# A mixture-of-experts block on one core: statistics and centred rows one step further ahead, and one product moved from DVE to POOL

## The chip, the cores and the metric

The kernel runs on one core of a Trainium2 chip, as one launch. The metric is the time of that launch on the device in microseconds (us). Engines are called as in the profile: PE (matrix products and transposes), DVE (vector), ACT (scalar), POOL (GpSimd), SP (only issues transfers).

## The reference, cut to what matters

The input x is 16 blocks of 512 rows of 256 numbers, all fp32. Each block has its own modulation rows, six of 256 numbers, made from a condition row.

```
mod = silu(c) @ wmod                       # sa, ca, ga, sb, cb, gb; |ga|, |gb| at least 0.25
h   = layernorm(x) * (1 + ca) + sa
x   = x + ga * linear_attention(h)         # causal, q and k through elu + 1, heads of 64
h   = layernorm(x) * (1 + cb) + sb         # the second modulation
n   = layernorm(h, rn_g, rn_b)
top two of 8 experts from n @ router_w.T + router_b, softmax over the two
x   = x + gb * sum of the two experts' gelu networks (256 -> 1024 -> 256) on layernorm(h)
```

So each row passes three layer norms: of x, of x after the attention, and of h. Each needs a mean and an inverse root of the variance.

## The kernel before

The work has two stages. The **routing stage** makes attention, second modulation and router choice for the 16 blocks and scatters the normed rows into lists, one list for each expert. The **expert stage** runs through 71 tiles of up to 256 listed rows. The diff touches the setup and the routing stage.

Each engine has its own instruction stream in a fixed order that is written out by hand, and the streams meet only in semaphores. The routing stage is a software pipeline (`pipeline`, L273) of 21 steps. In step i the engines work on several blocks: block i is projected (`project`), block i-1 gets its attention (`attend`), block i-2 the statistics of its new rows (`settle`), block i-3 the second modulation (`norm`), block i-4 its router scores and choice (`route`), block i-5 its places in the lists and the scatter (`place`). A helper pipeline beside it splits the experts' weights into two bf16 parts; in odd steps DVE makes the rest of the first weights (L940), in even steps that of the second (L946).

**Statistics.** DVE makes them in three groups: group 0 for the raw rows of block i+1, group 1 for block i-2 after attention, group 2 for the modulated rows of block i-3. For each there is `bn_stats` (L771) and `bn_aggr` (L779); one instruction adds epsilon for all groups (`ve`, L786), POOL raises it to the power -0.5 (`rs`, L544), and DVE makes the negative mean times that (`nm`, L803). ACT then writes the centred and scaled rows (`normalise`, L628): `xc` of block i at the head of its step, `xn2` of block i-3 and the normed rows of block i-4. PE transposes `xc` (L1322), ACT modulates it while it copies it from PSUM (`hT`, L664), and PE projects it (L1355).

**Second modulation.** DVE multiplies `xn2` by a broadcast row (L901, 128 partitions x 1024 elements), then adds another row (L908) and makes the statistics of group 2.

**Choice and places.** DVE finds the two best scores, makes two masks from them (`oh`, L1006) and their sum (`ohs`, L1009). PE sums the masks to ranks (L1341 to L1345). DVE adds the base (`cnt`, L1046), multiplies by the masks (`pick`, L1052), sums (L1059) and casts to `slot` (L1064). POOL issues eight indirect transfers for each block (L551), four ahead of the inverse root and four behind it. At the head of its step POOL makes `wog`, the output weights times a modulation row (L559, 64 partitions x 256 elements).

**Order on DVE in a step.** Wait for `nm`; statistics of group 1; ranks, picks and slots; the diagonal masks of the attention strips (`diag`, L886); statistics of group 0; the modulation product and sum; statistics of group 2; `ve`; the feature map (`phi`, L926), the running sum (`scan`, L930) and a product (`qz`, L932); `nm`; the rests of the weights; the new rows `x2` (L968); the choice.

**Loads.** SP loads block i+2 of x in step i (`load_x`, L364), blocks 0 and 1 at the start. All blocks of x stay in SBUF through the routing stage.

Of the kernel before, what the change touches and what calls it, by code (L numbers as in the profile page):

```python
# [23 lines left out]
P = 128  # L24
# [28 lines left out]
def adaln_moe_kernel(nc, x_d, wq_d, wk_d, wv_d, wo_d, rng_d, rnb_d, rw_d, rb_d, lng_d, lnb_d,  # L53
# [6 lines left out]
    with ctx:  # L60
# [192 lines left out]
        def used(i):  # L253

            if not isinstance(i, int):
                return slice(0, 3)
            return slice(0 if i < NB else 1 if i - 3 < NB else 2, 1 if i < 3 else 2 if i < 4 else 3)
# [30 lines left out]
        def _(sp):  # L288
            sp.dma_start(cin[:, :], c_d).then_inc(got_c, 16)
# [14 lines left out]

            sp.wait_ge(mod_step, 8)
# [58 lines left out]
            def load_x(i, half, r):  # L364
                if isinstance(i, int):
                    if i + 2 < NB:
                        sp.wait_ge(got_x[r], 16 * (half + 1))
                        sp.dma_start(resid[:, (i + 2) * NC:(i + 3) * NC, :], x_v[i + 2]).then_inc(got_x[r], 16)
                else:
                    sp.wait_ge(got_x[r], 16 * half + 16)  # L370
                    sp.dma_start(resid[:, ds((i + 2) * NC, NC), :], x_v[ds(i + 2, 1)]).then_inc(got_x[r], 16)
# [120 lines left out]
        def _(pool):  # L492
# [42 lines left out]
            def inverse_root(i, r):  # L535

                pool.wait_ge(ve_s, i + 1)

                wait_past(pool, xc_s, upto(i - 1))
                wait_past(pool, xn2_s, upto(i - 4))  # L540
                wait_past(pool, nrm_s, upto(i - 5))
                wait_past(pool, nm_s, i - 1)
# [73 lines left out]
        def _(act):  # L616
# [13 lines left out]

            def step(i, half, r, project, attend, settle, norm, route, place):
                if project or norm or route:
                    act.wait_ge(nm_s, i + 1)
                if project:
                    act.wait_ge(got_x[r], 16 * half + 16)
                    wait_past(act, xT_s, i)
                    normalise(lambda c: xc[:, c, :], rows(i), r, 0, xc_s)
# [4 lines left out]
                if project and r == 1:  # L642
                    act.wait_ge(b1p_s, half + 1)
                    wait_past(act, b1_out, 32 * half)
                    hold(act, "act")
                    a.activation(b1rows, Q[0:H + 1, :], ACT.Copy).then_inc(b1r_s, 1)
                if norm:
# [9 lines left out]
                if project:  # L657

                    act.wait_ge(xT_s, i + 1)
                    act.wait_ge(modc_s, i + 1)  # L660
                    wait_past(act, proj_s, i)
                    hold(act, "act")
                    for k in range(NK):
                        last = a.activation(hT[:, k, :], TR[k][:, :], ACT.Identity,  # L664
                                            bias=modc[:, r, 2 + k:3 + k], scale=modc[:, r, k:k + 1])
                    last.then_inc(hT_s, 1)
# [88 lines left out]
        def _(dve):  # L755
# [32 lines left out]
            def stats_before(i):  # L788

                if not isinstance(i, int):  # L790
                    return 3 * i - 4
                return min(i + 1, NB) + min(max(i - 2, 0), NB) + min(max(i - 3, 0), NB)

            def neg_mean_rstd(i, r):

                dve.wait_ge(rs_s, i + 1)

                wait_past(dve, xc_s, upto(i - 1))
# [23 lines left out]
            var_eps(0, 1)  # L822
# [32 lines left out]
            dve.wait_ge(rb_ps, 1)  # L855
            dve.wait_ge(got_r, 32)
            dve.wait_ge(base_set, 1)
            v.tensor_tensor(rbias[:, :], rbias[:, :], S[1][:, 0:E], ALU.add).then_inc(setup_done, 1)
            dve.wait_ge(setup_done, 1)

            v.tensor_copy(lge[:, :], lngb[:, 0, :]).then_inc(lge_s, 1)

            def step(i, half, r, project, attend, settle, norm, route, place):
                taken = stats_before(i)
                dve.wait_ge(nm_s, i + 1 if not isinstance(i, int) else min(i + 1, NB + 4))
                if settle:
                    dve.wait_ge(x2_s, i - 1)
                    hold(dve, "dve")
                    stats(rows(i - 2), 1)
                if place:  # L870
# [16 lines left out]
                if project and not (isinstance(i, int) and i == NB - 1):  # L887
                    if r == 0:
                        dve.wait_ge(got_x[1], 16 * half + 16)
                    else:  # L890
                        dve.wait_ge(got_x[0], 16 * half + 32)
                    hold(dve, "dve")
                    stats(rows(i + 1), 0)
                if norm:

                    b, q = i - 3, 1 - r
                    dve.wait_ge(got_cs[q], 16 * (half if q == 0 else half - 1))
                    dve.wait_ge(xn2_s, b + 1)
                    wait_past(dve, nrm_s, b - 1)
                    hold(dve, "dve")  # L900
                    v.tensor_tensor(h2[q], xn2, csB[:, q, D:2 * D].unsqueeze(1).to_broadcast([P, NC, D]), ALU.mult).then_inc(h2m_s, 1)  # L901
                if project and not (isinstance(i, int) and i == NB - 1):
                    moments(0, taken)
                    taken = taken + 1
                if norm:
                    b, q = i - 3, 1 - r
# [26 lines left out]
                if project or attend or norm:  # L933
                    neg_mean_rstd(i + 1, 1 - r)
# [12 lines left out]

                if attend:
# [312 lines left out]
        def _(pe):  # L1261
# [27 lines left out]
            def router_bias():  # L1289
# [5 lines left out]
                pe.wait_ge(setup_done, 1)  # L1295
# [8 lines left out]
            def step(i, half, r, project, attend, settle, norm, route, place):  # L1304
# [214 lines left out]
```

## Time and profile before

| | us |
|---|---|
| three runs | 1122.92, 1125.62, 1125.95; median 1125.62 |
| the profiled execution | 1125.48 |
| its span | 1123.6 |

| engine | busy us | share of the span |
|---|---|---|
| PE | 988.9 | 88% |
| DVE | 889.1 | 79% |
| POOL | 573.6 | 51% |
| ACT | 542.9 | 48% |

The shares are means over two unlike stages. The routing stage takes the first third of the span and the expert stage, in which PE is nearly always busy, the rest. The granted clock of PE is a mean of 0.92 of full speed, with 0.8 to 0.9 in most slices of the routing stage. A row of a timeline has the start in us from the span's start, the duration in us, the engine, the line, the operation, what it writes and reads, and how many instructions are merged; brackets give the engine's idle time before it and what ended it.

### The profile page before, as it was taken

The numbers are of one execution on the slowest core, as the hardware profiler recorded it, in microseconds if no ns is written. First come the engines' busy times: TensorE is split into PE (matmuls) and PEld (weight loads), VectorE is DVE, ScalarE is ACT, GpSimd is POOL, SyncE is SP. The second block draws the span as 40 slices with busy tenths as digits, with TensorE's granted clock in tenths as the row PEclk, the third lists the DMA queues.
The fourth block names the chain that finished last, engine by engine and source line by source line (L and its number), as shares of the span: only waits on it lengthen the run. The fifth ranks groups of instructions, "written<-read, shape, count | busy, mean of one in ns | idle before, by whom it ended". The sixth has DMA issues, their size and how long they took to land.

```text
span 1123.6 us, 31567 instructions
## 1 busy us (share of the span) xinstructions
PE 988.9 (88%) x8116; PEld 806.3 (72%) x8117; DVE 889.1 (79%) x3010; ACT 542.9 (48%) x1123; POOL 573.6 (51%) x478
## 2 busy tenths in 40 slices
PE   5777879887945099999999999999999999999997
PEld 1334545554534088888888888888888888888875
DVE  5578999999985567777877877877877877877776
ACT  1668787878843134434444443444443443444443
POOL 2121666666667536655455445445445445545543
PEclk8798888888965599999999999999999999999999
DMA  4465777876869466665565555566555556566453
GB/s 134 133 227 194 237 230 260 291 271 212 315 233 401 122 185 132 137 123 92 96 118 98 106 112 104 98 109 99 94 108 103 90 108 108 87 120 122 88 100 49
DMA packets 162626, 169.80 MB, mean 151 GB/s; under 512 B 89340, under 2 KB 136968, under 8 KB 158472
## 3 DMA queue, kind: packets, MB, share of 16 engines
q1 hardware_dynamic: 129736, 114.24, 36.5%
q0 software_dynamic: 32832, 54.88, 25.3%
q8 instruction: 25, 0.41, 0.2%
q14 instruction: 33, 0.27, 0.1%
HBM read 94.67 MB, written 62.78 MB: 140 GB/s over the span
## 4 chain that ended last, share of the span: by engine, by line
PE 66%; issue 8%; DVE 8%; POOL 6%; ACT 2%; DMA 1%; POOLq 0%; DVEq 0%; SPq 0%; ACTq 0%
PE banks L1440 32%; PE banks L1452 31%; POOL lists L551 5%; PE banks L1334 2%; DVE st L771 2%; POOL rs L544 2%; DVE store L968 1%; PE banks L1322 1%; ACT rowbuf L628 1%; DVE mv L779 1%; ACT store L712 1%; DVE rowbuf L908 1%; DMA out<-rowbuf,ydst 0%; DVE store L926 0%; DVE ix L1001 0%
## 5 line engine op out<-in xcount | busy, mean ns | idle before, releaser
L1440 PE MATMUL banks<-nhl,store 128*128 128x256 bf16 (+1 forms) x3408 | 450.5, 268 | 28.0 <-DMA nhl<-xhl 24.8
L740 ACT ACTIVATE gf<-banks,b1t 128x256 f32<-128x256 f32 (+1 forms) x568 | 263.0, 463 | 429.1 <-PE banks L1440 411.7
L1452 PE MATMUL banks<-store 128*128 x3240 | 448.0, 273 | 0.5
L1440 PEld LDWEIGHTS banks<-nhl,store 128*128 x3408 | 324.1, 98 | 71.0 <-issue 30.1
L587 POOL DMA_INDIRECT out<-rowbuf,ydst x135 | 223.7, 1657 | 294.1 <-DVE rowbuf L1222 222.0
L1452 PEld LDWEIGHTS banks<-store 128*128 128x128 bf16 x3240 | 310.5, 98 | 41.9 <-issue 1.8
L1231 DVE CAST store<-gf 128x256 bf16<-128x256 f32 (+1 forms) x568 | 180.5, 318 | 130.7 <-ACT gf L740 99.3
L1233 DVE TENSOR_TENSOR store<-gf,store 128x256 bf16<-128x256 f32 (+1 forms) x568 | 234.7, 413 | 19.5
L551 POOL DMA_INDIRECT lists<-store,slot x128 | 141.0, 1102 | 96.3 <-issue 49.0
L578 POOL DMA_INDIRECT store<-y_rows,ygb x135 | 135.2, 1001 | 63.3 <-issue 51.8
L544 POOL TENSOR_TENSOR rs<-ve,mhalf 128x12 f32<-128x12 f32 (+2 forms) x20 | 39.0, 1950 | 84.6 <-DVE ve L786 84.5
L628 ACT ACTIVATE rowbuf<-store,nm,rs 128x256 f32<-128x256 f32 x128 | 66.1, 588 | 23.5 <-DVE nm L803 23.3
L1222 DVE SCALAR_TENSOR_TENSOR rowbuf<-rowbuf,yw,store 128x256 f32<-128x256 f32 x135 | 59.4, 479 | 0.2 <-DVE rowbuf L1212 0.2
L1322 PE MATMUL banks<-ident,rowbuf 128*128 128x128 f32 x128 | 25.1, 360 | 31.8 <-ACT rowbuf L628 31.8
L1334 PE MATMUL banks<-store,vT 64*128 64x512 f32 (+3 forms) x128 | 38.4, 662 | 16.5 <-DVE store L968 8.5
L1183 DVE TENSOR_TENSOR xhl<-rowbuf,xhl 128x512 bf16<-128x512 f32 (+1 forms) x71 | 46.6, 658 | 7.7 <-ACT xhl L731 7.7
L731 ACT ACTIVATE xhl<-rowbuf 128x512 bf16<-128x512 f32 (+1 forms) x71 | 42.6, 600 | 18.4 <-DMA rowbuf<-lists 18.4
L1212 DVE TENSOR_TENSOR rowbuf<-banks,b2t 128x256 f32<-128x256 f32 x135 | 50.8, 416 | 0.7 <-PE banks L1452 0.7
L1322 PEld LDWEIGHTS banks<-ident,rowbuf 128*128 128x128 f32 x128 | 19.7, 183 | 41.1 <-ACT rowbuf L628 39.5
L771 DVE BATCH_NORM_STATS2 st<-store 128x6 f32<-128x256 f32 x128 | 44.8, 412 | 2.3 <-DMA store<-in_L_attn_x 2.0
L1355 PE MATMUL banks<-store,wqk 128*128 128x512 f32 x64 | 42.0, 790 | 3.0 <-ACT store L664 3.0
L1334 PEld LDWEIGHTS banks<-store,vT 64*128 64x128 f32 x128 | 23.2, 276 | 27.6 <-issue 24.5
(225 smaller groups left out, 970.0 us busy)
## 6 DMA issues: line engine op xcount, KB each, us to landing
rowbuf<-lists SPq DMA_DIRECT2D x64, 264.0 KB
store<-in_L_ffn_w SPq DMA_DIRECT2D x16, 1024.0 KB, 6.0
wsplit<-store SPq DMA_DIRECT2D x16, 1024.0 KB, 5.7
store<-wsplit SPq DMA_DIRECT2D x16, 1024.0 KB, 11.1
b2t<-in_L_ffn_b SPq DMA_DIRECT2D x71, 128.0 KB
store<-in_L_attn_x SPq DMA_DIRECT2D x16, 512.0 KB, 9.6
out<-store SPq DMA_DIRECT2D x16, 512.0 KB, 9.9
csB<-mod_rows SPq DMA_DIRECT2D x16, 256.0 KB, 4.0
```

The source lines that it names most:

```text
L544: g.tensor_tensor(rs[:, r, n, :], ve[:, n, :], mhalf[:, n, :], ALU.pow).then_inc(rs_s, 1)
L551: g.indirect_dma_start(list_d, bass.IndirectOffsetOnAxis(ap=slot[:, b % NR, t, c:c + 1], axis=0), nrm[:, b % NR, c, :], None).then_inc(sca ...
L578: g.indirect_dma_start(gbr[:, r, h, :], None, y_d[GBROW:GBROW + NB, :], bass.IndirectOffsetOnAxis(ap=ygb[:, r, h:h + 1], axis=0)).then_inc ...
L587: g.indirect_dma_start(out_rows, bass.IndirectOffsetOnAxis(ap=ydst[:, r, h:h + 1], axis=0), yt[:, r, h, :], None, compute_op=ALU.add).then ...
L628: last = a.activation(out(c), src(c), ACT.Identity, bias=nm[:, r, n, c:c + 1], scale=rs[:, r, n, c:c + 1])
L740: a.activation(gf[:, c % 2, 0:halves(j) * P], MM[c % 2][:, 0:halves(j) * P], ACT.Gelu, bias=b1t[:, r, c:c + 1]).then_inc(gf_s, 1)
L771: last = v.bn_stats(st[:, n, c, :], src(c))
L1231: v.tensor_copy(gh[:, c, cols], gf[:, c % 2, cols]).then_inc(gh_s, 1)
L1233: v.tensor_tensor(gl[:, c, cols], gf[:, c % 2, cols], gh[:, c, cols], ALU.subtract).then_inc(gl_s, 1)
L1334: last = t.matmul(SC[s], vT[at, q, s // 2 * P:(s // 2 + 1) * P], q_of[at, q, s * P:T], start=True, stop=True)
L1440: last = t.matmul(MM[c % 2][:, 0:halves(j) * P], w, nhl[:, r, m, 0:halves(j) * P], start=n == 0, stop=n == 5)
L1452: last = t.matmul(ACC[r][h][:, 0:D], g[:, c, h * P:(h + 1) * P], w, start=c == 0 and n == 0, stop=c == NI - 1 and n == 2)
```

## The change

Five things are edited.

1. In step i DVE makes the group 0 statistics of block i+2 (before: i+1), and it does so right behind those of group 1, ahead of ranks and slots. Setup makes two sets, for blocks 0 and 1. The counts in the waits go up by one.
2. ACT writes `xc` of block i+1 in step i, behind the attention output. It modulates and copies `hT` ahead of the wait for `nm`, and writes `xn2` behind it. Setup writes `xc` of block 0, and step 0 that of block 1.
3. POOL makes the modulation product, between `wog` and the first four scatters. It waits for `xn2` and for `ohs` of DVE's previous step. DVE keeps the sum (L908).
4. DVE makes `nm` behind the rests of the weights instead of ahead of them.
5. SP loads blocks 2 and 3 in setup and block i+3 in step i. The sum of the router's bias leaves the setup and is made in step 0; PE waits for it in step 1.

```diff
@@ sync
+            for b in range(2, 4):
+                load_block(b)
             sp.wait_ge(mod_step, 8)
...
             def load_x(i, half, r):
+                if 0 < i < NB - 3:
+                    load_block(i + 3)
@@ gpsimd
             def inverse_root(i, r):
-                pool.wait_ge(ve_s, i + 1)
+                pool.wait_ge(ve_s, i + 2)
...
+            inverse_root(-1, 1)
             inverse_root(0, 0)
...
+                if norm:
+                    b, q = i - 3, 1 - r
+                    pool.wait_ge(got_cs[q], 16 * (half if q == 0 else half - 1))
+                    pool.wait_ge(xn2_s, b + 1)
+                    wait_past(pool, nrm_s, b - 1)
+                    wait_past(pool, ohs_s, i - 4)
+                    hold(pool, "pool")
+                    g.tensor_tensor(h2[q], xn2, csB[:, q, D:2 * D].unsqueeze(1).to_broadcast([P, NC, D]), ALU.mult).then_inc(h2m_s, 1)
                 if place:
@@ scalar
+            def centred(b, r):
+                act.wait_ge(got_x[b % 2], 16 * (b // 2) + 16)
+                wait_past(act, xT_s, b)
+                normalise(lambda c: xc[:, c, :], rows(b), r, 0, xc_s)
+            act.wait_ge(nm_s, 1)
+            centred(0, 1)
...
+                if project:
+                    act.wait_ge(xT_s, i + 1)
...
+                    last.then_inc(hT_s, 1)
+                if i + 1 < NB or norm or route:
+                    act.wait_ge(nm_s, i + 2)
                 if norm:
...
+                if i == 0:
+                    centred(1, 0)
...
+                if 0 < i < NB - 1:
+                    centred(i + 1, r)
@@ vector
-            var_eps(0, 1)
+            var_eps(-1, 1)
+            dve.wait_ge(got_x[1], 16)
+            dve.wait_ge(mv_s, 1)
+            hold(dve, "dve")
+            stats(rows(1), 0)
+            neg_mean_rstd(-1, 1)
+            dve.wait_ge(nm_s, 1)
+            dve.wait_ge(ve_s, 1)
+            moments(0, 1)
+            var_eps(0, 2)
             dve.wait_ge(mod_ps, 1)
...
                     stats(rows(i - 2), 1)
+                if i + 2 < NB:
+                    dve.wait_ge(got_x[r], 16 * half + 32)
+                    hold(dve, "dve")
+                    stats(rows(i + 2), 0)
                 if place:
...
-                    stats(rows(i + 1), 0)
                 if norm:
                     b, q = i - 3, 1 - r
                     dve.wait_ge(got_cs[q], 16 * (half if q == 0 else half - 1))
-                    dve.wait_ge(xn2_s, b + 1)
-                    wait_past(dve, nrm_s, b - 1)
-                    hold(dve, "dve")
-                    v.tensor_tensor(h2[q], xn2, csB[:, q, D:2 * D].unsqueeze(1).to_broadcast([P, NC, D]), ALU.mult).then_inc(h2m_s, 1)
...
-                if project or attend or norm:
-                    neg_mean_rstd(i + 1, 1 - r)
+                if i == 0:
+                    router_bias()
                 if project and r == 1:
...
                     v.tensor_tensor(wbuf[:, 0, 6144:8192], w2f, wbuf[:, 0, 4096:6144], ALU.subtract).then_inc(rest2_s, 1)
 
+                if project or attend or norm:
+                    neg_mean_rstd(i + 1, 1 - r)
@@ tensor
-                pe.wait_ge(setup_done, 1)
...
+                    if b == 0:
+                        pe.wait_ge(setup_done, 1)
```

## Rows read from the trace of the kernel before

**Rows 1.** The table by stretches of time: length, each engine's busy us, PE clock.
```profile
112.00:302.00 190.00, 157.81 (x908) 100.41 (x908) 179.37 (x674) 151.22 (x304) 122.35 (x100) 0.85 0.77 259
...
383.00:1123.60 740.60, 718.81 (x6648) 634.33 (x6648) 575.52 (x1832) 298.53 (x639) 375.44 (x286) 0.99 0.58 107
```

**Rows 2.** The timeline of POOL: start us, us, what, idle time before.
```profile
1.96 0.16 POOL L500 IOTA experts<- 128x8 f32 x1
...
113.32 1.20 POOL L551 DMA_INDIRECT lists<-store,slot  x1 [10.25 <-issue]
...
208.15 1.00 POOL L551 DMA_INDIRECT lists<-store,slot  x1 [4.92 <-DVE slot L1064]
209.46 1.72 POOL L551 DMA_INDIRECT lists<-store,slot  x1 [0.30 <-issue]
...
214.22 2.30 POOL L544 TENSOR_TENSOR rs<-ve,mhalf 128x12 f32<-128x12 f32 x1 [0.39 <-DVE ve L786]
...
222.57 0.73 POOL L559 TENSOR_TENSOR wog<-wo,gaB 64x256 f32<-64x256 f32 x1
226.75 1.00 POOL L551 DMA_INDIRECT lists<-store,slot  x1 [3.45 <-DVE slot L1064]
...
240.17 0.74 POOL L559 TENSOR_TENSOR wog<-wo,gaB 64x256 f32<-64x256 f32 x1
...
302.96 1.44 POOL L551 DMA_INDIRECT lists<-store,slot  x1 [4.01 <-issue]
...
321.24 1.76 POOL L551 DMA_INDIRECT lists<-store,slot  x1 [4.87 <-DVE slot L1064]
...
338.07 1.27 POOL L551 DMA_INDIRECT lists<-store,slot  x1 [3.59 <-DVE slot L1064]
...
350.15 1.11 POOL L551 DMA_INDIRECT lists<-store,slot  x1 [0.30 <-issue]
```

**Rows 3.** The timeline of DVE in a full even step.
```profile
206.12 0.19 DVE L1046 TENSOR_TENSOR cnt<-banks,base 128x32 f32<-128x32 f32 x1 [0.62 <-PE banks L1345]
...
206.35 0.22 DVE L1052 TENSOR_TENSOR pick<-oh,cnt 128x64 f32<-128x64 f32 x1
...
207.82 1.40 DVE L771 BATCH_NORM_STATS2 st<-store 128x6 f32<-128x256 f32 x4
209.13 1.21 DVE L901 TENSOR_TENSOR rowbuf<-rowbuf,csB 128x1024 f32<-128x1024 f32 x1
210.26 0.37 DVE L779 BATCH_NORM_AGGREGATE mv<-st 128x2 f32<-128x6 f32 x4
```

**Rows 4.** All instructions of line 559: shortest, median, longest in ns.
```profile
L559 POOL TENSOR_TENSOR wog<-wo,gaB x16: 723/742/1385, 35.4 to 315.6; 64x256 f32<-64x256 f32 x16
```

**Rows 5.** The timeline of DVE: two mask sums and one scan.
```profile
203.59 0.19 DVE L1009 TENSOR_TENSOR ohs<-oh 128x32 bf16<-128x32 f32 x1
...
214.84 1.22 DVE L930 TENSOR_TENSOR_SCAN zT<-onesf,store 64x512 f32<-64x512 f32 x1
...
222.72 0.64 DVE L1009 TENSOR_TENSOR ohs<-oh 128x32 bf16<-128x32 f32 x1
```

**Rows 6.** The timelines of ACT, PE and DVE in the first steps.
```profile
17.93 2.08 ACT L628 ACTIVATE rowbuf<-store,nm,rs 128x256 f32<-128x256 f32 x4 [14.97 <-DVE nm L803]
...
30.16 0.63 ACT L688 ACTIVATE ex<-ex 128x512 f32<-128x512 f32 x1
...
20.16 1.94 PE L1322 MATMUL banks<-ident,rowbuf 128*128 128x128 f32 x8 [1.51 <-ACT rowbuf L628]
...
38.00 1.97 PE L1322 MATMUL banks<-ident,rowbuf 128*128 128x128 f32 x8 [0.60 <-ACT rowbuf L628]
...
32.44 0.68 DVE L926 SCALAR_TENSOR_TENSOR store<-banks,ex 128x512 f32<-128x512 f32 x1
...
74.35 0.69 DVE L886 TENSOR_TENSOR store<-store,causal 128x512 f32<-128x512 f32 x1 [1.56 <-ACT store L672]
...
92.91 0.69 DVE L886 TENSOR_TENSOR store<-store,causal 128x512 f32<-128x512 f32 x1 [1.93 <-ACT store L672]
```

More of the change, by code:

```diff
@@ L256, in used @@
                 return slice(0, 3)
-            return slice(0 if i < NB else 1 if i - 3 < NB else 2, 1 if i < 3 else 2 if i < 4 else 3)
+            return slice(0 if i + 1 < NB else 1 if i - 3 < NB else 2, 1 if i < 3 else 2 if i < 4 else 3)
         def halves(j):
@@ L288, in _, with load_block @@
         def _(sp):
+            def load_block(b):
+                sp.wait_ge(got_x[b % 2], 16 * (b // 2))
+                sp.dma_start(resid[:, b * NC:(b + 1) * NC, :], x_v[b]).then_inc(got_x[b % 2], 16)
             sp.dma_start(cin[:, :], c_d).then_inc(got_c, 16)
@@ L364, in load_x @@
             def load_x(i, half, r):
[L365 to L371, printed above, removed]
+                if 0 < i < NB - 3:
+                    load_block(i + 3)
             def load_w1(e):
@@ L629, in normalise @@
                 last.then_inc(done, 1)
-            def step(i, half, r, project, attend, settle, norm, route, place):
[L632 to L637, printed above, removed]
+            def centred(b, r):
[4 more added lines that the diff above has]
+            centred(0, 1)
+            def step(i, half, r, project, attend, settle, norm, route, place):
                 if attend:
@@ L646, in step @@
                     a.activation(b1rows, Q[0:H + 1, :], ACT.Copy).then_inc(b1r_s, 1)
+                if project:
+                    act.wait_ge(xT_s, i + 1)
+                    act.wait_ge(modc_s, i + 1)
+                    wait_past(act, proj_s, i)
+                    hold(act, "act")
+                    for k in range(NK):
+                        last = a.activation(hT[:, k, :], TR[k][:, :], ACT.Identity,
+                                            bias=modc[:, r, 2 + k:3 + k], scale=modc[:, r, k:k + 1])
+                    last.then_inc(hT_s, 1)
+                if i + 1 < NB or norm or route:
+                    act.wait_ge(nm_s, i + 2)
                 if norm:
@@ L656, in step @@
                     a.activation(dex[:, :], dl[:, :], ACT.Exp).then_inc(dex_s, 1)
[L657 to L666, printed above, removed]
+                if i == 0:
+                    centred(1, 0)
                 if attend:
@@ L788, in stats_before @@
             def stats_before(i):
-                if not isinstance(i, int):
-                    return 3 * i - 4
-                return min(i + 1, NB) + min(max(i - 2, 0), NB) + min(max(i - 3, 0), NB)
+                return min(i + 2, NB) + min(max(i - 2, 0), NB) + min(max(i - 3, 0), NB)
             def neg_mean_rstd(i, r):
-                dve.wait_ge(rs_s, i + 1)
-                wait_past(dve, xc_s, upto(i - 1))
+                dve.wait_ge(rs_s, i + 2)
+                wait_past(dve, xc_s, upto(i))
                 wait_past(dve, xn2_s, upto(i - 4))
@@ L854, in _, with router_bias @@
             v.tensor_copy(ef[:, 0, 0:1], base[:, 0:1]).then_inc(base_set, 1)
-            dve.wait_ge(rb_ps, 1)
-            dve.wait_ge(got_r, 32)
             dve.wait_ge(base_set, 1)
-            v.tensor_tensor(rbias[:, :], rbias[:, :], S[1][:, 0:E], ALU.add).then_inc(setup_done, 1)
-            dve.wait_ge(setup_done, 1)
+            hold(dve, "dve")
             v.tensor_copy(lge[:, :], lngb[:, 0, :]).then_inc(lge_s, 1)
+            def router_bias():
+                dve.wait_ge(rb_ps, 1)
+                dve.wait_ge(got_r, 32)
+                v.tensor_tensor(rbias[:, :], rbias[:, :], S[1][:, 0:E], ALU.add).then_inc(setup_done, 1)
+                dve.wait_ge(setup_done, 1)
             def step(i, half, r, project, attend, settle, norm, route, place):
                 taken = stats_before(i)
-                dve.wait_ge(nm_s, i + 1 if not isinstance(i, int) else min(i + 1, NB + 4))
+                dve.wait_ge(nm_s, min(i + 2, NB + 5))
                 if settle:
@@ L869, in step @@
                     stats(rows(i - 2), 1)
+                if i + 2 < NB:
+                    dve.wait_ge(got_x[r], 16 * half + 32)
+                    hold(dve, "dve")
+                    stats(rows(i + 2), 0)
                 if place:
@@ L886, in step @@
                     v.tensor_tensor(diag, diag, causal[:, :].unsqueeze(1).to_broadcast([P, NC, P]), ALU.mult).then_inc(diag_s, 1)
[L887 to L891, printed above, removed]
-                    hold(dve, "dve")
-                    stats(rows(i + 1), 0)
                 if norm:
@@ L897, in step @@
                     dve.wait_ge(got_cs[q], 16 * (half if q == 0 else half - 1))
-                    dve.wait_ge(xn2_s, b + 1)
-                    wait_past(dve, nrm_s, b - 1)
-                    hold(dve, "dve")
-                    v.tensor_tensor(h2[q], xn2, csB[:, q, D:2 * D].unsqueeze(1).to_broadcast([P, NC, D]), ALU.mult).then_inc(h2m_s, 1)
-                if project and not (isinstance(i, int) and i == NB - 1):
+                if i + 2 < NB:
                     moments(0, taken)
@@ L905, in step @@
                 if norm:
-                    b, q = i - 3, 1 - r
                     dve.wait_ge(h2m_s, b + 1)
```

4 lines of the change are left out of this document (2 added, 2 removed).

## The prediction

> **What bounds the kernel now.** I read the table by stretches first. The last 740 us are the expert stage, where PE is busy 97% of the time at the full clock; nothing of the change lies in it [rows 1]. The change can only move its start, so I look for the time of the last scatter. In the stretch of the full batch steps, 112 to 302 us, DVE is busy 179 of 190 us, PE 158, ACT 151 and POOL 122 [rows 1]. DVE is thus the engine that sets the pace, and the reader is to see in the timelines where the others wait for it. POOL starts a step's scatters at 113.32 in the first step that has any and at 302.96 ten steps later, so 18.96 us a step [rows 2]. Between them it waits 4.92 and 3.45 us for DVE's slots, in an even and an odd step [rows 2]. From one wait to the end of the next wog product POOL needs 15.15 us in the even step (208.15 to 223.30) and 14.16 us in the odd one (226.75 to 240.91), 14.66 in the mean [rows 2]. So POOL has 4.2 us a step to spare, and that is the whole room for a new POOL product.
>
> **Taking the product from DVE.** L901 starts at 209.13 and the next DVE instruction 1.13 us later: 1.13 us less DVE work in 16 steps [rows 3]. DVE also waits 0.62 us for PE's ranks in even steps [rows 3]; with the statistics of the block after next put ahead of the ranks (1.31 us from start to start [rows 3]) that wait is filled, some 0.3 us a step. DVE alone could then do a step in 18.96 - 1.13 - 0.31 = 17.5 us, and in 17.2 when the wog product no longer falls on its mask sums (next paragraph).
>
> **What POOL pays.** wog is 64x256 and takes 0.723 us at least, 0.742 in the median and 1.385 at most over 16 [rows 4]. The new product has 1024 elements in each partition, four times as many. If all of 0.742 goes by element it takes 2.97 us. An IOTA of 8 elements takes 0.16 us [rows 2], which is about what an instruction costs in itself: (0.742 - 0.16) x 4 + 0.16 = 2.5 us, my value. The lower end is the DVE's own 1.21 us [rows 3], the upper four times the longest wog, 5.5 us. *GPSIMD Engine Reference* in the Trainium skill, section 3.1, gives 4497 ns for a two-input product of 2048 elements, about 2.3 us for half of it; no run here shows that size yet, and by it the sum below would fall by 0.2 us a step.
>
> **The wait that comes with it.** With room 4.2 and price 2.5 the product seems free, but the two engines hold each other up. ohs, a sum of two SBUF inputs, takes 0.19 us at 203.59 with POOL idle and 0.64 us at 222.72, and then it ends at 223.36, 0.06 after the wog product (222.57 to 223.30) [rows 2, 5]. So DVE's two-input operation waits until POOL's product is over. The other way round, POOL's second scatter takes 1.72 us instead of about 0.96, and it starts in the middle of L901 [rows 2, 3]. The new product is released by ohs. Behind it on DVE come two small copies and both sets of statistics, which have one input each, and then pick, which has two. From ohs to pick that is 2.76 us in the step shown (203.59 to 206.35 [rows 3, 5]), less 0.62 of waiting, plus 1.31: about 3.4, or 3.2 from the end of ohs. A product that starts at once ends at 2.6 and disturbs nobody. A late one holds pick. From the start of pick to the first scatter it is 1.80 us (206.35 to 208.15) [rows 2, 3]. POOL's circle is then: 0.1 to start, 2.5 for the product, 1.8 for pick, slots and the way to POOL, and POOL's own work. That work is 14.66 less the 0.39 us in which the power waited for ve [rows 2] (in the new order ve is ready first), less about 0.35 because L946 stands elsewhere (its hold on the scatters falls in even steps only), plus 0.2 because L908 now falls on the first scatter from its beginning: 14.1, bounds 13.9 and 14.7. The circle is 18.5 us, longer than DVE's 17.2. If the product started at once, POOL would be done at 3.2 + 1.8 + 14.1 = 19.1 us after ohs, 1.9 us too late for a step of 17.2; so from the second such step on it does come late, pick is held by about 1.3 us a step, and POOL's circle sets the pace. Ten steps of 18.96 become ten of 18.5: 4.6 us gained, instead of the 17 that DVE's busy time promises. The other cuts on DVE disappear in the hold.
>
> *SBUF — State Buffer* in the Trainium skill, section Who interferes with whom, says of this that a DVE operation with two SBUF inputs and a POOL operation that reads SBUF exclude each other for the whole instruction. The ohs row agrees. The scan at 214.84 does not: it has two SBUF inputs, lies inside the power of 2.30 us at 214.22 and takes 1.22 us all the same [rows 2, 5]. The measurement decides, so the hold is certain for a product with many elements only as far as wog shows it.
>
> **The early steps.** Here DVE is not full and a chain is cut. ACT centres block 0 only when DVE has gone through the modulation rows, and PE stands until 20.16 for it; ACT has then waited 14.97 us for nm [rows 6]. With the centring released before those rows, PE starts behind its own transposes, 1.5 us earlier (PE's wait ahead of 20.16 is 1.51). ex is ready at 30.16 + 0.63 = 30.8, but DVE takes it at 32.44 because it is making statistics [rows 6]; these move into DVE's idle time before, another 1.6. PE's wait of 0.60 for xc at 38.00 goes [rows 6]. In the steps at 53 and 63 us the chain runs through x2 and the scores and I count nothing. In the two steps with the product but without scatters (diag at 74.35 and 92.91) DVE waits 1.56 and 1.93 us for the strips [rows 6]; the 1.31 us of statistics fit there, and 1.13 go to POOL, which is idle: 2.44 twice, 4.9. Sum 1.5 + 1.6 + 0.6 + 4.9 = 8.6. At the first scatter step the statistics stand ahead of the slots and cost 1.31 - 0.62 = 0.7. First scatter 7.9 us earlier; ends: 5 if ACT or PE is late next in the two middle steps, 10 if wog's holds on DVE go there as well. Blocks 2 and 3 are loaded some 15 us earlier, into a stretch where the queue waits for the modulation rows; I give that nothing. The router bias sum moves behind step 0's work and PE waits for it only in step 1, nothing either.
>
> **The end.** The last scatters are POOL's chain: starts at 302.96, 321.24, 338.07, 350.15 [rows 2]. The product falls in the first two waits: the first interval is 18.28 with a wait of 4.87, so POOL works 13.4; plus 0.1 + 2.5 + 1.8 is 17.8, so -0.5. The second is 16.83 with a wait of 3.59, 13.2 of work, 17.6 with the product, +0.8. Ahead of 350.15 POOL has only the 0.30 us that lie ahead of every scatter, so the third costs its whole 2.5. Sum +2.8. Moving nm behind the weight remainders frees DVE while POOL raises the power, but POOL's queue sets the end, so nothing.
>
> **The sum.** -7.9 - 4.6 + 2.8 = -9.7, and with the holds of wog in the early steps (up to 2, I take 1) -10.7. The profiled execution takes 1125.48 for a span of 1123.6, and the median of the runs is 1125.62, the same within 0.2. Forecast 1115.
>
> **Rivals.** *DVE sets the pace.* The product doesn't hold pick, or only in part, as the power doesn't hold the scan. Then a step is 17.2, POOL needs 0.1 + 2.5 + 14.1 = 16.7 and fits: -7.9 - 17.6 + 2.5 = -23, 1103. For it speaks DVE's 179 of 190 us, against it the 0.64 us of ohs. *Nothing moves.* The product takes 2.97 and both old delays of the scatters stay: 0.1 + 2.97 + 1.8 + 14.66 = 19.5, +5.7 in ten steps, +4.3 at the end, -7.9: +2, 1127 at worst and 1123 if only one of them holds. *Slower: a slow POOL product.* Place: between ohs and pick, in every step from the second scatter step on. Each us over 2.5 costs ten steps and three at the end, 13 us in all, so it decides from 2.5 + 10/13 = 3.3 us on. At 4.0 us it gives 1115 + 19 = 1134, at 5.5, four times the longest wog, 1154. For it: wog's 1.385 when DVE holds it up; against it: its median lies at its minimum, and the stretch after ohs has no two-input operation. *The early gain is not there*: the steps with centring ahead have another late input; then -2, 1123.
>
> **Chances.** Forecast (1108 to 1121) 0.55, DVE sets the pace 0.17, nothing moves or no early gain 0.16, slower by the slow product 0.12. The range 1100 to 1127 leaves out the slow product and the best of the DVE case. A change of 0.3% (3.4 us) is about what a measurement here can tell: faster 0.75, the same 0.12, slower 0.13.
>
> **What would show it.** Right: POOL's new product near 2.5 us; its start later than ohs by 1 us or more in the full steps; pick drawn out to about a us or more and ending just after the product; scatter starts 18.5 us apart; first scatter near 105.5; PE without a wait for xc. Wrong: scatter starts 17.2 apart with pick at 0.2 us (first rival), or a product over 3.3 us (the slower one). DVE's busy time falls by about 16 x 1.13 = 18 us less the holds in every case and proves nothing.

## The result: slower by 0.6%, and the profile after

The kernel after takes 1131.88 us (median of 4 runs, 1127.96 to 1133.22), the kernel before 1124.41 us (4 runs, 1122.92 to 1125.95): ratio 1.0061, 95% interval 1.0044 to 1.0077. I had forecast 1115, so the sign was wrong, and the time lies outside the range. The profiled execution of after is its fastest one, 1127.96 us with a span of 1126.2; the rows below explain +2.6 us of span, and the end of this section says what the slower runs have in addition.

The table by stretches (length, busy us of PE, PEld, DVE, ACT and POOL with their instructions, PE clock, busy share of the DMA engines, GB/s):
```profile
112.00:302.00 190.00, 154.99 (x865) 96.14 (x865) 170.01 (x632) 146.71 (x293) 152.84 (x108) 0.82 0.73 251
...
383.00:1126.20 743.20, 718.65 (x6648) 634.22 (x6648) 575.91 (x1835) 298.49 (x639) 377.30 (x288) 0.99 0.59 107
```
Beside [rows 1], DVE has 9 us less and POOL 30 us more, of which ten products explain 24: POOL's other instructions have grown too. The expert stage is as long as before. The first scatter stands at 106.63 instead of 113.32 (-6.7), from it to the first scatter ten steps later it is 194.52 us instead of 189.64 (+4.9), and from there to the first expert matmul 95.87 instead of 91.36 (+4.5). Together +2.7. The rows are of after, and the last one is of before:
```profile
106.63 2.04 POOL L554 DMA_INDIRECT lists<-store,slot  x1 [2.22 <-issue]
...
301.15 1.75 POOL L554 DMA_INDIRECT lists<-store,slot  x1 [1.67 <-DVE slot L1087]
...
397.02 4.39 PE L1464 MATMUL banks<-nhl,store 128*128 128x256 bf16 x24 [24.56 <-DMA nhl<-xhl]
```
```profile
394.32 4.47 PE L1440 MATMUL banks<-nhl,store 128*128 128x256 bf16 x24 [24.82 <-DMA nhl<-xhl]
```

Where the ten steps lose, the timeline of POOL shows (start us, us, instruction, idle time before); it answers to [rows 2]:
```profile
184.29 2.01 POOL L554 DMA_INDIRECT lists<-store,slot  x1 [1.74 <-DVE slot L1087]
...
190.56 2.30 POOL L546 TENSOR_TENSOR rs<-ve,mhalf 128x12 f32<-128x12 f32 x1
...
198.59 2.36 POOL L570 TENSOR_TENSOR rowbuf<-rowbuf,csB 128x1024 f32<-128x1024 f32 x1
202.69 2.01 POOL L554 DMA_INDIRECT lists<-store,slot  x1 [1.74 <-DVE slot L1087]
...
208.95 4.41 POOL L546 TENSOR_TENSOR rs<-ve,mhalf 128x12 f32<-128x12 f32 x1
...
219.09 2.36 POOL L570 TENSOR_TENSOR rowbuf<-rowbuf,csB 128x1024 f32<-128x1024 f32 x1
223.19 2.01 POOL L554 DMA_INDIRECT lists<-store,slot  x1 [1.74 <-DVE slot L1087]
...
229.46 3.40 POOL L546 TENSOR_TENSOR rs<-ve,mhalf 128x12 f32<-128x12 f32 x1
```
The circle is there: product 2.36, then 1.74 until DVE's slots let the next scatter start, then POOL's own work until the next product. From 184.29 to 202.69 it is 18.40 us, my 18.5. From 202.69 to 223.19 it is 20.50, and nearly all of the difference is one instruction: the power of 12 elements takes 4.41 us instead of 2.30. Four of the ten intervals are 20.5 with a power of 4.41; four are 18.2 to 18.4; one odd step has a power of 3.40 and 19.51; and in the last interval, 19.55, the power is one of 8 elements and takes 3.78 where the unheld ones take 1.67. Ten times 18.4 would be 184.

The timeline of DVE at the same time, which answers to [rows 3, 5]:
```profile
190.51 2.55 DVE L961 SCALAR_TENSOR_TENSOR store<-store,lge 128x1024 bf16<-128x1024 f32 x2
...
196.56 0.19 DVE L1032 TENSOR_TENSOR ohs<-oh 128x32 bf16<-128x32 f32 x1
...
197.07 2.71 DVE L791 BATCH_NORM_STATS2 st<-store 128x6 f32<-128x256 f32 x8
199.70 0.17 DVE L1069 TENSOR_TENSOR cnt<-banks,base 128x32 f32<-128x32 f32 x1
199.79 1.20 DVE L1051 TENSOR_SCALAR d<-dex 128x4 f32<-128x4 f32 x1
200.90 0.21 DVE L1075 TENSOR_TENSOR pick<-oh,cnt 128x64 f32<-128x64 f32 x1
...
202.65 1.19 DVE L929 TENSOR_TENSOR rowbuf<-rowbuf,csB 128x1024 f32<-128x1024 f32 x1
...
208.19 0.69 DVE L953 TENSOR_TENSOR store<-store,zT 64x512 f32<-64x512 f32 x1
208.91 2.29 DVE L967 TENSOR_TENSOR store<-store 128x2048 bf16<-128x2048 f32 x1
...
229.41 2.48 DVE L961 SCALAR_TENSOR_TENSOR store<-store,lge 128x1024 bf16<-128x1024 f32 x2
```
L967, the rest of the second weights (the remainder of the even steps; L961 is that of the odd ones), starts at 208.91, the power at 208.95. The power ends at 213.36, 2.16 us after the remainder, so nearly all of its 2.3 us of work came after the remainder was over. In the odd step L961 starts at 190.51 and the power at 190.56, and here the power is at its 2.30 and L961 the one that is drawn out a little: its two pieces take 2.55 us, and 2.48 at 229.41, where the power is the one of 3.40. That power was held by the first piece (1.1 us) and not by the second. L929 starts at 202.65 and stretches the scatter of 202.69 to 2.01 us. The two engines meet in this way in every step, since L953 holds the fourth scatter (207.56, 1.37 us for 0.96) until DVE is through with it, and the power and the remainder then start in the same moment.

The end, POOL again:
```profile
322.49 3.07 POOL L554 DMA_INDIRECT lists<-store,slot  x1 [0.30 <-issue]
...
349.65 2.37 POOL L570 TENSOR_TENSOR rowbuf<-rowbuf,csB 128x1024 f32<-128x1024 f32 x1
352.18 2.04 POOL L554 DMA_INDIRECT lists<-store,slot  x1 [0.17 <-issue]
```
The product at 349.65 costs its whole length, as foreseen (the interval before 352.18 is 14.50 for 12.08). Not foreseen: a scatter of 3.07 us, which falls on L967 of the last step that has it (322.42 to 324.71), and one of 2.04, which falls on L929 (it starts at 352.12). An undisturbed scatter takes 0.96.

The start of the first steps, PE and DVE, answering to [rows 6]:
```profile
18.03 1.97 PE L1344 MATMUL banks<-ident,rowbuf 128*128 128x128 f32 x8
...
27.69 0.69 DVE L947 SCALAR_TENSOR_TENSOR store<-banks,ex 128x512 f32<-128x512 f32 x1 [0.62 <-ACT ex L706]
```
PE starts 2.1 us earlier and DVE takes ex 4.75 us earlier.

The other executions take up to 1133. Part of that is more long powers in odd steps: the profile of a repeat (after_again, span 1128.9, +2.7) has two of 3.4 us instead of one. Its ten intervals take 1.2 us more, the way from there to the first expert matmul 0.5, the expert stage 0.8, and its first scatter is at 106.78. The 4 us between the profiled execution and the median are thus explained in part only.

In the four traces with this order on DVE (after, its two repeats and rest2_stt below) the remainder starts 0.03 to 0.06 us ahead of the power at every meeting. The even one (L967) holds the power in 20 of 20, the odd one (L961) in 8 of 24. rest2_stt, in which both have the same form, has the same split, so it isn't the form; why they differ stays open.

### The profile page after: what moved, and what is told of

Its sections match the earlier page's. It is cut to its first block, busy times and chain, and to the rows that moved or that the text cites. A ratio compares the mean times of both kernels' runs of the same rounds, so it can differ in the third digit from the quotient of the medians.

```text
span 1126.2 us, 31567 instructions
## 1 busy us (share of the span) xinstructions
PE 987.9 (88%) x8116; PEld 803.7 (71%) x8117; DVE 885.4 (79%) x2996; ACT 544.5 (48%) x1123; POOL 624.5 (55%) x495
## 4 chain that ended last, share of the span: by engine, by line
PE 64%; DVE 12%; POOL 8%; issue 6%; DMA 1%; ACT 1%; POOLq 0%; DVEq 0%; SPq 0%; ACTq 0%
PE banks L1464 31%; PE banks L1476 31%; POOL lists L554 5%; POOL rs L546 3%; DVE st L791 3%; DVE store L991 2%; DVE d L1051 1%; DVE store L961 1%; PE banks L1358 1%; DVE zT L951 1%; DVE ix L1024 1%; DVE rowbuf L929 0%; DVE mv L799 0%; DVE mx L1014 0%; DMA out<-rowbuf,ydst 0%
## 5 line engine op out<-in xcount | busy, mean ns | idle before, releaser
L554 POOL DMA_INDIRECT lists<-store,slot x128 | 144.5, 1129 | 57.6 <-issue 32.5
L546 POOL TENSOR_TENSOR rs<-ve,mhalf 128x12 f32<-128x12 f32 (+2 forms) x21 | 50.3, 2396 | 49.3 <-DVE ve L806 48.9
L570 POOL TENSOR_TENSOR rowbuf<-rowbuf,csB 128x1024 f32<-128x1024 f32 x16 | 37.8, 2361 | 20.9 <-ACT rowbuf L639 12.2
L1379 PE MATMUL banks<-store,wqk 128*128 128x512 f32 x64 | 45.8, 856 | 1.8 <-ACT store L668 1.8
L1431 PE MATMUL banks<-wog,store 128*128 128x257 f32 x128 | 38.9, 458 | 3.6 <-ACT store L719 3.6
```

Source lines behind the costliest of these rows:

```text
L554: g.indirect_dma_start(list_d, bass.IndirectOffsetOnAxis(ap=slot[:, b % NR, t, c:c + 1], axis=0), nrm[:, b % NR, c, :], None).then_inc(sca ...
```

## Experiments

The theory from this profile, H: a two-input operation of DVE and a POOL instruction that reads SBUF exclude each other; whoever is first makes the other wait. The product on POOL isn't slow, but it leaves POOL so little room that the power always meets the remainder. Rivals: the order of remainder and nm does it (O), the form of the remainder's instruction (F), something that only accompanies the long power, as PE's clock or transfers (C).

**The same kernel again, twice.**

> The changed kernel once more, to see what differs between its executions. Theory H (held operations): in even steps POOL's power waits behind the rest of the second weights (2.29 us, both inputs in SBUF), so it takes 4.41 us instead of 2.30; in odd steps power and the first piece of the rest of the first weights start within 50 ns of each other, and either may win, which is 1.1 us a step. So the scatter intervals alternate near 18.4 and 20.5 us, and more of the odd ones are 19.5 in a slower execution: 1128 to 1134 us, about 1131.5. Rival C (clock and transfers: PE's granted clock is 0.82 in the full steps instead of 0.85, and the loads come earlier): a slower execution has a lower clock and longer PE stretches, with the same intervals of the power.

> The kernel after, unchanged, so that the two runs behind it have it on their own chip. 1.004 to 1.008 of the kernel before; power 4.4 us in even steps; intervals 20.5 (even) and 18.4 or 19.5 (odd).

1130.46 us, ratio 1.0054 (1.0042 to 1.0066), and 1131.46, 1.0065 (1.0046 to 1.0084). The even intervals are 20.5 and the even powers 4.41 in both; in the second the first scatter is later too (108.21).

**nm ahead of the remainders again.**
```diff
+ if project or attend or norm: neg_mean_rstd(i + 1, 1 - r)   # ahead of the remainders, as in before
- if project or attend or norm: neg_mean_rstd(i + 1, 1 - r)   # behind them
```

> The changed kernel with nm ahead of the weight rests again (edit 4 undone). Theory H: the power is no longer held (2.30 us in all steps), but DVE now waits for it before the rests, so the rests fall behind it, hold one of the last four scatters by up to 1 us in even steps, and delay x2 and the mask sums by 2.3 us in odd steps. The product then waits for the mask sums; interval 19.4 in the mean as now, 1131 us (1127 to 1136). Rival O (edit 4 alone is what costs): the power at 2.30 us gives 2.1 us back in each even step, 10 to 12 us in all, 1120 us.

1133.94 us, 1.0090 (1.0075 to 1.0105): slower still, O falls. POOL and DVE:
```profile
212.59 2.30 POOL L546 TENSOR_TENSOR rs<-ve,mhalf 128x12 f32<-128x12 f32 x1
...
216.43 1.91 POOL L554 DMA_INDIRECT lists<-store,slot  x1 [0.30 <-issue]
```
```profile
215.07 0.22 DVE L821 SCALAR_TENSOR_TENSOR nm<-mv,rs 128x12 f32<-128x12 f32 x1 [2.55 <-POOL rs L546]
215.22 2.29 DVE L969 TENSOR_TENSOR store<-store 128x2048 bf16<-128x2048 f32 x1
```
All full powers are 2.30 now, but DVE stands still for 2.55 us for each, and the remainder falls on a scatter instead. Intervals are 19.2 to 20.7.

**The product back on DVE, all else as after.**
```diff
- g.tensor_tensor(h2[q], xn2, csB[...], ALU.mult).then_inc(h2m_s, 1)   # POOL, behind ohs
+ v.tensor_tensor(h2[q], xn2, csB[...], ALU.mult).then_inc(h2m_s, 1)   # DVE, where before has it
```

> The changed kernel with the modulation product back on DVE in its old place; all else of the change stays. Theory H: POOL has room again, the power starts when ve is ready and is over before the weight rests, so 2.30 us; d is not drawn out. DVE sets the pace at about 18.96 less 0.3 for the filled rank wait, 18.6; first scatter at 106.6 + 2.3 = 109; the end as before. -4.4 - 3.5 = -8: 1117 us, faster than before. Rival C: the product's place has nothing to do with it, the loss stays: 1126 to 1132 us.

1119.61 us, 0.9951 (0.9939 to 0.9964): faster than before. The other edits are good for 5 us, and the product's move takes away 11. POOL:
```profile
181.48 1.76 POOL L554 DMA_INDIRECT lists<-store,slot  x1 [2.86 <-DVE slot L1083]
...
187.16 3.02 POOL L546 TENSOR_TENSOR rs<-ve,mhalf 128x12 f32<-128x12 f32 x1
```
and DVE:
```profile
186.86 1.22 DVE L947 TENSOR_TENSOR_SCAN zT<-onesf,store 64x512 f32<-64x512 f32 x1
```
POOL waits again, 2.86 us here, and so starts its power at another point of DVE's step: it is held 0.7 us, by the scan, and not 2.1 (I had expected no hold at all). Seven of the ten intervals are 17.8 to 18.4. In the longest one, 20.57, DVE waits 1.53 us for PE, whose granted clock is 0.75 there; that step is long through PE and not through POOL.

**The remainder in another form.**
```diff
- v.tensor_tensor(rest2, w2f, rounded, ALU.subtract)
+ v.scalar_tensor_tensor(rest2, w2f, 1.0, rounded, ALU.mult, ALU.subtract)
```

> The changed kernel with the rest of the second weights as one scalar_tensor_tensor (w2 times 1.0, minus the head) instead of a tensor_tensor; same two inputs in SBUF, same size. Theory H: any operation with two SBUF inputs holds the power, the form doesn't matter and only who is first: power 4.4 us as now in even steps, 1131 us. Theory F (the form matters: the rest of the first weights is a scalar_tensor_tensor and left the power at 2.30 in three of four odd steps): power 2.30 in even steps, 5 x 2.1 us less in ten steps and 1 to 2 at the end, 1119 us. Rival C: 1131 us.

1129.64 us, 1.0044 (1.0028 to 1.0060), the even power 4.42 us, interval 20.5. F falls.

**The product alone, in the kernel before**, on two chips.
```diff
- v.tensor_tensor(h2[q], xn2, csB[...], ALU.mult).then_inc(h2m_s, 1)
+ g.tensor_tensor(h2[q], xn2, csB[...], ALU.mult).then_inc(h2m_s, 1)   # on POOL, behind wog and ohs
```

> The kernel before, with nothing but the modulation product moved to POOL behind ohs. The power begins ahead of the scan and 2.7 us ahead of the remainder in the kernel before, so theory H expects no long hold there unless the engines shift against each other by those 2.7 us: POOL's circle is 0.1 + 2.4 + 1.8 + 14.1 to 14.7 = 18.4 to 19.0 us, the end costs 2.8 to 4.5, the first scatter is 1 to 2 us earlier: 1123 to 1130, between no change and slower. If the product's move alone is what makes the power fall together with the remainder (a phase that the circle forces on the two engines, whatever the order of the statistics), the power takes 4.4 us in some steps here too, and it is 1130 or more.

> The same kernel as product_alone, where the expert stage has its usual length. From its trace: last scatter at 388.1, 6.5 us behind that of the kernel before, nearly all of it in the last six steps (85.9 instead of 78.6 us), so 1.004 to 1.006 of the kernel before. A theory in which only the order of the statistics does the harm: 1.000 or less.

On the first of these chips the expert stage is longer (the kernel before takes 1154.15 us there), and I use only the traces up to the first expert matmul from it. There: 1154.65 us, 0.9993 (0.9977 to 1.0010). On the second: 1127.63 us, 1.0026 (1.0017 to 1.0035), less than the 1.004 expected. The full powers are 2.30 but for one of 3.03, and the ten steps take 187.68 us, 2.0 less than before: without the new order of the statistics the power starts ahead of the remainder and isn't held. The loss is at the end: from the first scatter ten steps on to the last scatter of all it is 85.6 us instead of 78.6 (that one is at 385.12 instead of 381.59). So the product alone costs 0.3% (nothing on the first chip), the rest alone gains 0.5%, and both together lose 0.5 to 0.7%: the sum of the two would be a gain of 0.2%, and some 0.8% comes from their meeting. The three ratios are from different chips, so the 0.8 is rough.

**The remainders in pieces of 512 elements**, on the same two chips (after ran on the second only).
```diff
- v.tensor_tensor(rest2[0:2048], ...)
+ for n in range(4): v.tensor_tensor(rest2[n * 512:(n + 1) * 512], ...)   # L961's two likewise in halves
```

> The kernel after, with the weight remainders cut: the two scalar_tensor_tensor of 1024 elements into four of 512, the tensor_tensor of 2048 into four of 512; same work, same order. Theory H (POOL's power and DVE's remainder, which start in the same moment, exclude each other; whoever is first makes the other wait to its end): the power then waits for one piece of some 0.55 us and no longer for 2.1, so it takes at most 2.9 us in even and odd steps, the scatter starts of the full steps are 18.4 to 19.0 us apart in both parities, and the time is 8 to 10 us under the kernel after, 1120 to 1123. Rival K (DVE keeps its place over instructions that follow each other without a gap): the power still takes 4.4 us in even steps and 1131 stays. Rival C (the even steps are long for another reason, PE's clock or a transfer, and the long power is a symptom): the power gets short and the even intervals stay near 20.5.

> The same kernel as rests_in_pieces (weight remainders in pieces of 512 elements), on a chip on which the expert stage has its usual length. Theory H: full steps of 18.4 to 19.0 us instead of 20.5 and 18.4 to 19.5 by turns, so 7 to 10 us under the kernel after, 0.997 to 1.000 of the kernel before. Theory C (the length of a step is set elsewhere): within 2 us of the kernel after.

1150.40 us, 0.9964 (0.9947 to 0.9981), and 1127.50, 1.0028 (1.0014 to 1.0041). Beside after on the second chip (1131.46) that is 4 us, not 7 to 10. POOL and then DVE of the second:
```profile
162.00 2.37 POOL L570 TENSOR_TENSOR rowbuf<-rowbuf,csB 128x1024 f32<-128x1024 f32 x1
168.95 2.01 POOL L554 DMA_INDIRECT lists<-store,slot  x1 [4.58 <-DVE slot L1093]
...
184.96 2.35 POOL L570 TENSOR_TENSOR rowbuf<-rowbuf,csB 128x1024 f32<-128x1024 f32 x1 [1.14 <-issue]
...
213.78 2.82 POOL L546 TENSOR_TENSOR rs<-ve,mhalf 128x12 f32<-128x12 f32 x1
```
```profile
160.66 3.76 DVE L1012 COPY lge<-lngb 128x4 f32<-128x4 f32 x1
...
185.00 2.40 DVE L1081 TENSOR_TENSOR pick<-oh,cnt 128x64 f32<-128x64 f32 x1
...
213.75 2.51 DVE L971 TENSOR_TENSOR store<-store 128x512 bf16<-128x512 f32 x4
```
The power at 213.78 waits for one piece, 0.5 us, and gets its turn between two: H, not the rival by which DVE keeps its place. From 188.97 on the steps are 18.56 and 18.94 by turns, with the power at 2.30 and 2.82, which is the forecast's circle; the interval follows the power, and C falls. The gain is lost ahead of that, in steps of 21.38 and 20.02: a COPY of 4 elements takes 3.76 us in the first of them, through the last scatter, wog and the product, and everything behind it is late. In the second the product starts late itself (1.14 us of idle time before it) and holds pick for 2.40 us.

**Half of the product on each engine, remainders in pieces.**
```diff
- g.tensor_tensor(h2[q], xn2, ...)
+ g.tensor_tensor(h2[q][:, 0:2, :], xn2[:, 0:2, :], ...)   # POOL
+ v.tensor_tensor(h2[q][:, 2:4, :], xn2[:, 2:4, :], ...)   # DVE
```

> As the run before, and of the modulation product only the first half (512 of 1024 elements) is made on POOL, the second on DVE behind ohs. Theory H: POOL's circle loses half of 2.36 us, about 1.2, DVE gains 0.6; a step then has some 17.4 us of POOL and 17.8 of DVE: intervals 17.8 to 18.2, the end cheaper by 3 times 1.2, in all 1114 to 1118, under the kernel before. A theory in which the product's length matters little because DVE or PE sets the pace anyway: the same as rests_in_pieces within 2 us.

A miss: 1154.32 us, 0.9998 (0.9981 to 1.0015), 4 us above the run with the whole product on POOL. POOL has time (it waits 4.59 us for the slots at 265.33), but DVE is held before it reaches them:
```profile
279.63 1.28 POOL L570 TENSOR_TENSOR rowbuf<-rowbuf,csB 128x512 f32<-128x512 f32 x1
```
```profile
278.39 2.56 DVE L1048 CAST store<-ix 128x4 f32<-128x4 uint32 x1
```
This cast ends at 280.95 and the half product at 280.91; between the cast's start and there POOL has wog (278.95, 0.74 us) and the half product, and the cast is held through both. In seven of the ten steps a cast or copy behind ohs takes 2.0 to 2.6 us; with the whole product (rests_in_pieces) that happens in one. The powers of the full steps are held too, at 2.9 to 3.0. That POOL meets the casts because the shorter product brings it to wog earlier is only argued.

**The remainders behind x2.**

```diff
- remainders, nm; den, lg, max, x2
+ den, lg, max, x2; remainders, nm      # the order on DVE
```

> The kernel after, with the weight remainders and nm moved behind the residual sum x2, so that DVE makes x2 while POOL raises the power. Theory H: the power is held by nothing or by the two pieces of x2 only, 2.30 to 3.0 us in every step; but the remainders come later and can hold a scatter (2.0 us more once in a step where one falls on it) and x2 comes 2.3 us earlier to PE. Intervals 18.4 to 19.5, time 1119 to 1127. Rival C: even intervals stay at 20.5 whatever the power takes.

1157.87 us, 1.0039 (1.0017 to 1.0060), no gain. The profiled execution is its fastest, 1151.39, so the rows show where a step's time goes but not what the median has in addition. POOL and DVE:
```profile
207.03 2.30 POOL L546 TENSOR_TENSOR rs<-ve,mhalf 128x12 f32<-128x12 f32 x1
209.52 2.91 POOL L554 DMA_INDIRECT lists<-store,slot  x1 [0.20 <-issue]
```
```profile
209.22 2.28 DVE L990 TENSOR_TENSOR store<-store 128x2048 bf16<-128x2048 f32 x1
```
The power is 2.30 in all full steps, and the interval here is still 20.28. That is C's number, but POOL's own instructions account for it: 2.11 less on the power, 1.95 more on the scatter on which the remainder now falls. POOL is busy throughout, and so the hold found a victim in each of the three places that the remainder has had.

**The product on POOL only while POOL is idle.**
```diff
- if norm:                  # POOL: product
+ if norm and i < 5:        # POOL: product; DVE makes it for i >= 5
```

> The kernel after with the product on POOL in the two steps that have no scatters (i < 5), and on DVE in the 14 others. Theory H: the product costs nothing where POOL is idle and a hold on its circle where it is not. First scatter as in the kernel after (106 to 107, 1.5 us before that of product_on_dve), intervals of 18.0 and 18.0 to 19.2 as in product_on_dve, the time 1 to 2 us under product_on_dve, 0.993 to 0.996 of the kernel before. If the early gain is lost again because DVE sets the pace of the first scatter steps: as product_on_dve, 0.995.

1113.88 us, 0.9909 (0.9889 to 0.9929): the best version, 11 us under before and 18 under after. First scatter at 105.37, eight of the ten intervals 17.8 to 18.4 and the others 18.6 and 20.9, and no product behind the last power. In the one of 20.9 DVE waits 1.69 us for PE at a granted clock of 0.76. POOL waits for DVE again:
```profile
216.94 1.76 POOL L554 DMA_INDIRECT lists<-store,slot  x1 [2.88 <-DVE slot L1092]
```
It is more than the 1 to 2 us over product_on_dve that I expected (another chip, ratios 0.9951 and 0.9909). 2.8 us of it are the first scatter (108.14 there), but 1.6 of these are there already when DVE takes ex of the third step (57.92 instead of 59.51), ahead of the first product, where the two kernels are the same; the product can account for the other 1.2. In the last intervals product_on_dve has 19.79 and 19.49 where this one has 17.79 and 16.71. The table by stretches for these two intervals, first of product_on_dve and then of this kernel:
```profile
293.39:313.18 19.79, 14.24 (x66) 10.82 (x66) 16.57 (x60) 11.69 (x25) 10.81 (x11) 0.57 0.63 225
313.18:332.67 19.49, 13.82 (x64) 11.29 (x64) 13.30 (x54) 7.26 (x16) 12.32 (x10) 0.50 0.67 225
```
```profile
289.69:307.48 17.79, 11.26 (x66) 8.55 (x66) 16.72 (x59) 11.66 (x25) 11.91 (x10) 0.72 0.62 211
307.48:324.19 16.71, 9.77 (x64) 8.01 (x64) 13.23 (x54) 7.26 (x16) 12.31 (x10) 0.70 0.83 304
```
The same PE work takes 14.24 us at a granted clock of 0.57 and 11.26 at 0.72; 0.50 is the lower of the two levels, 1.2 GHz. Why the one run got less clock there stays open. So of the 0.4% between the two versions only 1.2 us, 0.1%, has its cause shown; the gain over after (0.9909 and 1.0065 on the same chip) stands apart from that.

## Why the prediction was wrong

- *What bounds the kernel.* DVE, with room of 4.2 us on POOL: right, and it was the room that mattered. After, POOL sets the pace.
- *The product costs 2.5 us.* 2.36, at 16 of 16 places within 0.03. The figure of 4497 ns in *GPSIMD Engine Reference* in the Trainium skill, section 3.1, which the prediction names, is for an add; half of it, 2.25 us, is an estimate as near to the 2.36 as mine, on the other side. The slow product, my rival on the slower side, is not what happened.
- *The circle.* Right in form: product, slots, POOL's own work. It says 18.5, the odd steps have 18.4. The instruction that is held is `d`, which has one input, and not pick, but for one step (297.12, 2.46 us): the ten `d` have a median of 1206 ns, and 158 with the product on DVE. The sum is the same.
- *POOL's own work is 14.1, bounds 13.9 and 14.7.* **This step failed.** It is 14.30 in the odd steps (184.29 to 198.59) and 16.40 in the even ones (202.69 to 219.09). I had let it shrink by 0.35 us, since L946 "stands elsewhere"; instead the remainder, now L967, moved onto the power and holds it 2.1 us. Five such holds (four of 2.11, and 3.78 for 1.67) make 10.5 and the odd one 1.1, together 11.6. Without them the ten intervals would sum to 182.9, 2.1 under my 185.0: -4.6 + 11.6 - 2.1 = +4.9. That is 9.5 us over the forecast. The early steps are 2.2 over (-8.9 counted, with the 1 us for wog's holds, and -6.7 measured) and the end 1.7, together the way from -10.7 to the +2.7 of the profiled execution.
- *Why I let it pass.* I took the scan of [rows 5], which lies inside the power and isn't drawn out, as a case against the hold. But the power had begun first (214.22, the scan 214.84), and in the new order DVE is first. product_on_dve shows the difference with the same pair: scan at 186.86, power at 187.16, and the power takes 3.02. *SBUF — State Buffer* in the Trainium skill, section Who interferes with whom, which the prediction names, also says that issue order decides who blocks. The trace agrees where DVE is clearly first; with starts 0.03 to 0.06 us apart both outcomes occur.
- *The early steps, -7.9.* -6.7: near, but partly by luck. DVE takes ex 4.75 us earlier in step 0 and 5.2 earlier in the third step (forecast 3.1 and 3.7); the two steps with the product and no scatters then gain 3.2, not 4.9; and the first scatter step loses 1.8, not 0.7, since `d` is held there too (1.23 us at 103.22; in product_early_on_pool, without a product there, it takes 0.16 and the first scatter is 1.3 us earlier).
- *The end, +2.8.* +4.5. The third product is as priced (+2.4); the scatters of 3.07 and 2.04 us are holds that I hadn't counted (2.1 and 1.1). "POOL's queue sets the end, so nothing" was wrong for the order of remainder and nm, since the remainder now meets a scatter.
- *The rivals.* All four priced the product or the gain; none was a hold of DVE on POOL that appears only in the new phase. By number "nothing moves" (1127) is near the profiled execution, and the slow product at 3.8 us would give the median; both for reasons that the rows refute.

Behind it stands one error of method. I worked out the hold on DVE's side of the meeting and took POOL's own work from the old phase of the two engines. Where a change takes away the slack of an engine, its instructions move against those of the other, and each long two-input operation has to be laid against whatever POOL does at the new time.

## What to carry to other kernels

Work that moves from DVE to POOL is priced with the meetings it causes, on both sides, and not by its length: here the 2.36 us of product were as cheap as calculated, and cost 2.1 us more in every second step by what they did to the phase. Give POOL such work in the steps in which it is idle (worth 1.2 us here), and leave it its wait in the others: with the wait back, the power met only the scan, for 0.7 us. When a hold is moved by reordering, look for its next victim before claiming its price.

## What the runs showed of the hardware that I had not expected

- Which small DVE instructions a POOL product holds depends on their kind. Eight BATCH_NORM_STATS2 took 2.71 us beside wog and the product (197.07) and 2.71 us with POOL idle (197.41 in product_on_dve); a TENSOR_SCALAR, a CAST and a COPY of 4 elements, with one input each, were drawn out to 1.20, 2.56 and 3.76 us. *SBUF — State Buffer* in the Trainium skill, same section, says that copy, cast and tensor_scalar can use a mode with both port pairs and then contend with POOL; the trace agrees for these three.
- A power of POOL that has begun is not stopped by a two-input operation of DVE, nor does it stop one: the scan at 214.84 took 1.22 us inside the power of 2.30 at 214.22 [rows 2, 5]. One that starts while such an operation runs waits nearly to its end (4.41 where L967 of 2.29 us started 0.04 us before it, 3.02 where the scan of 1.22 us started 0.30 us before). So H, by which the two exclude each other, holds for the power with DVE first and not with POOL first; POOL's products do make DVE wait.
- Between the four pieces of a remainder, which follow each other without a gap, the power got in after the first (2.82 us). The COPY at 160.66 got in nowhere between a scatter, wog (161.32) and the product: it ended at 164.42, the product at 164.37. I did not test this by itself.
- A two-input operation of DVE holds the issue of an indirect DMA as it holds a power: 3.07 and 2.91 us for 0.96, beside remainders of 2.3.
